# Rounding two hidden rows per VectorE operation instead of one in the second matrix product of a post-norm block

## The reference

```
x = layernorm(x + ssm(x))                      # a diagonal complex state-space layer, 256 states
x = layernorm(x + ffn(x))

def ffn(x):
    h  = rmsnorm(x) * norm_w
    gv = act_quant(h) @ weight_quant(w_gv).T   # 2048 -> 2 x 8192
    value, gate = split(gv)
    h  = value * silu(gate)                    # 8192 wide
    return x + act_quant(h) @ weight_quant(w_out).T     # 8192 -> 2048

def act_quant(a):                              # per row (token)
    scale = 127 / max(|a|)
    return clip(round(a * scale), -127, 127) / scale
```

## Time and profile before

| what | value |
|---|---|
| median of the runs before | 5870.79 us (2 runs, 5864.95 to 5876.63) |
| the profiled execution, its own time | 5864.32 us |
| its span (slowest core, first to last instruction) | 5862.7 us |
| spans of the eight cores | 5836.2 to 5862.7 us |
| granted TensorE clock, mean over the span | 0.810 to 0.812 of full speed on all cores |
| PE busy | 3430.6 us (59%) |
| DVE busy | 2559.8 us (44%), 3497 instructions |
| ACT busy | 1404.7 us (24%) |
| POOL busy | 648.0 us (11%) |

### The profile page before, as it was taken

How to read it: one execution, slowest core, us unless ns; L and a number is a source line. 1 busy time by engine, 2 the same in 40 slices (tenths; PEclk the granted TensorE clock), 3 DMA queues, 4 the chain that set the end, 5 groups by cost and what they waited for, 6 DMA issues and landing times.

```text
span 5862.7 us, 43737 instructions; the slowest of 8 cores (5836.2 to 5862.7 us)
## 1 busy us (share of the span) xinstructions
PE 3430.6 (59%) x13489; PEld 1345.3 (23%) x13489; DVE 2559.8 (44%) x3497; ACT 1404.7 (24%) x1134; POOL 648.0 (11%) x805
## 2 busy tenths in 40 slices
PE   1223421403888787877877799737772574476273
PEld 0110000001333333333333344212231221122121
DVE  1331844746333333333333344487573466268101
ACT  2222122132444444444444433100000000000000
POOL 0210000000000000000000000001112211311314
PEclk9857765756999898988888899868896797788686
DMA  8223345365555455665565522124442443343333
GB/s 223 74 99 108 127 156 169 123 208 163 190 187 190 169 144 136 151 147 133 154 147 132 137 90 92 39 71 131 127 140 81 126 137 97 119 131 122 96 115 106
DMA packets 211695, 774.79 MB, mean 132 GB/s; under 512 B 24412, under 2 KB 61439, under 8 KB 161799
## 3 DMA queue, kind: packets, MB, share of 16 engines
q10 hardware_dynamic: 64512, 318.80, 16.5%
q0 software_dynamic: 68832, 243.32, 15.6%
q1 hardware_dynamic: 78120, 209.87, 12.3%
HBM read 662.83 MB, written 117.44 MB: 133 GB/s over the span
## 4 chain that ended last, share of the span: by engine, by line
DMA 33%; PE 23%; DVE 17%; ACT 11%; issue 10%; POOL 5%; DVEq 1%; ACTq 0%; POOLq 0%; SPq 0%
DMA WOF<-woutT 7%; PE psA L987 6%; DMA WR<-wq2sp 5%; DMA WR<-wgvL 5%; PE psA L784 5%; DMA WOF<-wgvL 5%; PE psB L784 5%; DMA wq2sp<-P 4%; ACT HBF L734 3%; DMA WR<-woutT 3%; ACT P L745 2%; ACT WR L748 2%; PE psB L987 2%; DVE HBF L796 2%; ACT MNA L730 2%
## 5 line engine op out<-in xcount | busy, mean ns | idle before, releaser
L987 PE MATMUL psA<-P,WR 128*128 128x512 bf16 x3072 | 766.3, 410 | 568.7 <-DMA WR<-wq2sp 461.6
L784 PE MATMUL psA<-P,CBF 128*128 128x512 bf16 x2048 | 512.2, 411 | 202.7 <-DVE CBF L738 193.1
L784 PE MATMUL psA<-P,MNA 128*128 128x512 bf16 x2048 | 508.1, 408 | 179.8 <-DVE MNA L738 170.2
L987 PEld LDWEIGHTS psA<-P,WR 128*128 128x128 bf16 x3072 | 308.5, 103 | 1043.2 <-issue 759.3
L784 PE MATMUL psB<-P,CBF 128*128 128x512 bf16 x2048 | 457.4, 379 | 9.6
L784 PE MATMUL psB<-P,MNA 128*128 128x512 bf16 x2048 | 457.4, 379 | 9.6
L752 DVE TENSOR_TENSOR P<-P,WR 128x2048 bf16<-128x2048 bf16 x64 | 78.4, 1225 | 680.7 <-ACT WR L748 680.7
L784 PEld LDWEIGHTS psA<-P,CBF 128*128 128x128 bf16 x2048 | 211.5, 104 | 502.0 <-issue 312.2
L784 PEld LDWEIGHTS psA<-P,MNA 128*128 128x128 bf16 x2048 | 210.1, 104 | 476.2 <-issue 283.7
L987 PE MATMUL psB<-P,WR 128*128 128x512 bf16 x1024 | 248.2, 402 | 82.9 <-DMA WR<-wq2sp 80.8
L398 ACT ACTIVATE WOF<-WOF 128x2048 f32<-128x2048 f32 x96 | 183.5, 1912 | 393.0 <-DMA WOF<-wgvL 252.8
(11 more groups left out here) (217 smaller groups left out, 4096.3 us busy)
## 6 DMA issues: line engine op xcount, KB each, us to landing
P<-wgvL SPq DMA_DIRECT2D x128, 1024.0 KB
WR<-wq2sp POOLq DMA_DIRECT2D x256, 512.0 KB, 4.0
WOF<-woutT ACTq DMA_DIRECT2D x96, 1024.0 KB, 6.2
WOF<-wgvL ACTq DMA_DIRECT2D x64, 1024.0 KB, 5.0
WR<-wgvL ACTq DMA_DIRECT2D x64, 1024.0 KB, 5.1
h2sp<-CBF POOLq DMA_DIRECT2D x128, 256.0 KB, 4.5
WR<-woutT ACTq DMA_DIRECT2D x32, 1024.0 KB, 5.0
wq2sp<-P POOLq DMA_DIRECT2D x64, 512.0 KB, 8.4
```

Source lines behind the costliest of these rows:

```text
L784: sv=sv, last=last: t.matmul(PS[:, (vg * 2 + tq) * 512:(vg * 2 + tq + 1) * 512], WQap(sv + vg)[:, a * 128:(a + 1) * 128], P1[:, a * T + th ...
L987: seg=seg, PSm=PSm: t.matmul(PSm(ds), WR[:, sl * 2048 + jj * 256 + ds * 128: sl * 2048 + jj * 256 + (ds + 1) * 128], P1[:, seg * 16384 + j ...
```

## The change

`d_chain` now takes two blocks, j and j + 1, and is called for every second j. The two DMAs and the two products stay at 512 columns each and are issued one behind the other (DMA, product, DMA, product); the products fill the two halves of one float buffer of 1024 columns. The five rounding operations then run once over 1024 columns. The scratch sets are new (`RNW`: halves of `MNA` and of `WOF`), and the integer copy and its float copy share one memory. `round_neg` is no longer called here. The feeder lists hold 16 pieces for the chains where they held 32, so `d_mm` spreads them and what follows them differently over the groups.

```diff
+    RNW = [
+        (MNA[:, 0:1024], R("MNA", 0, 1024),
+         MNA[:, 1024:2048].bitcast(I32), MNA[:, 1024:2048], R("MNA", 1024, 2048)),
+        (WOF[:, 0:1024], R("WOF", 0, 1024),
+         WOF[:, 1024:2048].bitcast(I32), WOF[:, 1024:2048], R("WOF", 1024, 2048)),
+    ]
+
     def d_chain(q, seg, j):
         par = q % 2
-        jo = seg * 32 + j
-        hq = jo % 8
-        hsl = j % 2
-        b.dma("sync", lambda s, q=q, jo=jo, hq=hq: s.dma_start(
...
-        round_neg(hsl,
-                  P1[:, seg * 16384 + j * 512:seg * 16384 + (j + 1) * 512],
...
+        src_ap, src_r, i_ap, cf_ap, ic_r = RNW[(j // 2) % 2]
+        for h in range(2):
+            jo = seg * 32 + j + h
+            hq = jo % 8
+            b.dma("sync", lambda s, q=q, jo=jo, hq=hq: s.dma_start(
+                out=CBF[:, hq * 512:(hq + 1) * 512],
+                in_=h2sp_t[:, jo, q * 512:(q + 1) * 512]),
+                reads=[("h2sp", jo, q // 2)],
+                writes=R("CBF", hq * 512, (hq + 1) * 512, es=2))
+            b.op("vector", lambda v, hq=hq, h=h, src_ap=src_ap, par=par:
+                 v.tensor_tensor(
+                src_ap[:, h * 512:(h + 1) * 512],
+                CBF[:, hq * 512:(hq + 1) * 512], S2B[par], OP.mult),
+                reads=R("CBF", hq * 512, (hq + 1) * 512, es=2) + S2R[par],
+                writes=src_r)
+        dst_ap = P1[:, seg * 16384 + j * 512:seg * 16384 + (j + 2) * 512]
+        dst_r = R("P1", seg * 16384 + j * 512, seg * 16384 + (j + 2) * 512, es=2)
+        b.op("vector", lambda v: v.tensor_copy(i_ap, src_ap),
+             reads=src_r, writes=ic_r)
+        b.op("vector", lambda v: v.tensor_copy(cf_ap, i_ap),
+             reads=ic_r, writes=ic_r)
+        b.op("vector", lambda v: v.tensor_tensor(src_ap, src_ap, cf_ap,
+                                                 OP.subtract),
+             reads=src_r + ic_r, writes=src_r)
...
     def d_quant(q, seg):
-        for j in range(32):
+        for j in range(0, 32, 2):
             d_chain(q, seg, j)
...
-        f0 = [(lambda q=q, j=j: d_chain(q, 1, j)) for j in range(32)] + tail
+        f0 = [(lambda q=q, j=j: d_chain(q, 1, j)) for j in range(0, 32, 2)] + tail
...
-            f1 = [(lambda q=q, j=j: d_chain(q + 1, 0, j)) for j in range(32)]
+            f1 = [(lambda q=q, j=j: d_chain(q + 1, 0, j)) for j in range(0, 32, 2)]
```

More of the change, by code:

```diff
@@ L935, in d_rowsQ @@
         bcast_row(dqrow, DQR[par], PSB(3), RB(3), DQB[par], DQR[par])
+    RNW = [
[4 more added lines that the diff above has]
+    ]
     def d_chain(q, seg, j):
         par = q % 2
-        jo = seg * 32 + j
-        hq = jo % 8
-        hsl = j % 2
-        b.dma("sync", lambda s, q=q, jo=jo, hq=hq: s.dma_start(
[L943 to L953, removed]
-        round_neg(hsl,
-                  P1[:, seg * 16384 + j * 512:seg * 16384 + (j + 1) * 512],
-                  R("P1", seg * 16384 + j * 512,
-                    seg * 16384 + (j + 1) * 512, es=2))
+        src_ap, src_r, i_ap, cf_ap, ic_r = RNW[(j // 2) % 2]
@@ L959, in d_quant @@
+        b.op("vector", lambda v: v.scalar_tensor_tensor(
+            cf_ap, src_ap, 0.5, cf_ap, OP.is_ge, OP.add),
+            reads=src_r + ic_r, writes=ic_r)
+        b.op("vector", lambda v, dst_ap=dst_ap: v.scalar_tensor_tensor(
+            dst_ap, src_ap, -0.5, cf_ap, OP.is_le, OP.subtract),
+            reads=src_r + ic_r, writes=dst_r)
     def d_quant(q, seg):
-        for j in range(32):
+        for j in range(0, 32, 2):
             d_chain(q, seg, j)
```

## The result

The changed kernel takes 6206.85 us (median of 11 runs) against 5863.4 (median of 10 runs of the kernel before on the same chips), a ratio of 1.0576 with a 95% interval of 1.0551 to 1.06. It is slower by 5.8%; 5.6% was forecast, and 6200 us.

A forecast was written before the change was run, and what follows sets the result against it. Bounds taken: VectorE in stage (0, 0), a loop of engines and weight loads in seg 1, VectorE then GpSimd's order in later stages. 44 + 51 + 84 + 150 = 329 us on 5864 gave 6193; forecast 6200, range 6105 to 6290.

The forecast's parts named there:

- The lag of the odd load: In each pair on VectorE, the second product waits for its load, requested only after the first product: 2.4 to 3.9 us.
- Stage (0, 0): First stage of the last part: VectorE stays the bound, 306 us against 262, +44 us.
- Chains of (q, 0): Stages q = 1 to 3: 18 pairs on VectorE take 177 us against 149, +84 us together.
- Seg 1: Groups of q = 0 to 2: VectorE becomes the bound, 31.0 us a group against 28.6, +51 us together.
- The feeder's split: Stages q = 1 to 3: `d_rowsL` stands behind four groups, not six, so two more come behind the wait: +150 us.
- Rival A: The odd load isn't held up, a pair takes 7.0 us, the new split still costs 150: 5925 us, chance 0.06.
- Rival B: The odd load's lag stays but the split costs nothing, GpSimd's batches overlapping with TensorE: 6050 us, chance 0.07.
- C: VectorE's gain of 1.1 us a pair is passed on in full, without lag or split cost: 5730 us, chance 0.03.
- D: Seg 1's lag of 3.9 us holds everywhere, a pair takes 10.8 us: 6290 us, chance 0.06.

The follow-up runs named there:

- loads_first: The changed kernel with both loads of a pair recorded ahead of both products, new split kept: 5912 us, ratio 1.0069 against the kernel before.
- slots_apart: The changed kernel with its recording order kept, CBF slots dealt out so that a pair's blocks share no region: 5915 us, ratio 1.0074 against the kernel before.
- before_new_split: The kernel before with two 512-column chains in each feeder piece, so the list has the changed kernel's length: 6022 us, ratio 1.0282.
- apply_loads_on_sp: The changed kernel with the apply pieces' loads issued by SP's queue instead of ScalarE's: 6086 us, ratio 1.0334 against the kernel before.
- weights_early: both_fixes_sp with each weight load recorded right behind the matmuls that free its half of WR: 5513 us, ratio 0.935 against the kernel before.
- both_fixes_sp: The changed kernel with a pair's loads first, the feeder's old split and the apply loads on SP: 5705 us, ratio 0.9678 against the kernel before.

## Why the prediction was right

- *The lag of the odd load* (2.4 to 3.9 us by stage, read from SP's waits for the even block): shown. On core 0 the 128 odd products wait 420 us; loads_first and slots_apart take the wait away and with it 295 and 292 us, some 4.7% of the changed kernel's time each. That the cause is the shared region, and not the load's place in the code, is shown by slots_apart.
- *Stage (0, 0)*, +44: measured +47.3. *Chains of (q, 0)*, +84: measured +81.2.
- *Seg 1*, +51: measured +41.4. The mechanism was right and the size a fifth too large. Three figures of that term were off on core 0. The forecast had 217 us for the seven intervals, 651 in three quarters, and 633.6 were measured. From the first addition of a group to the end of its last operation it took 9.5 us, read from one group in which VectorE waited 5.10 us for the residual's load; the changed kernel takes 8.2 on the mean of those 21 groups, 28 us less in all. For two pairs it had 21.6 us, and they take 22.1, 10 us more in all. And it took 200 us for the kernel before in each quarter, 600 in all, where 592.2 were measured. One group of the changed kernel, in the timeline of VectorE on core 0, from its first addition through its last operation to the next group's first addition:

```profile
4146.68 0.69 DVE L1040 TENSOR_TENSOR Z2S<-psA,P 128x512 f32<-128x512 f32 x1
...
4154.31 0.69 DVE L1050 SCALAR_TENSOR_TENSOR Z2S<-CBF,Z2S 128x512 f32<-128x512 f32 x1 [3.93 <-DMA CBF<-x1sp]
...
4177.05 0.68 DVE L1040 TENSOR_TENSOR Z2S<-psB,P 128x512 f32<-128x512 f32 x1
```

The wait of the last operation of a group, in the waits of the kernel before from 3300 us on (sum, count, longest):

```profile
DVE Z2S L1032 <- DMA CBF<-x1sp: 146.6, 32, 6.5
```

The same of the changed kernel from 3700 us on:

```profile
DVE Z2S L1050 <- DMA CBF<-x1sp: 120.4, 32, 5.0
```

The mean over the 32 groups fell from 4.6 us to 3.8. Why this load comes sooner behind the addition was not tried.
- *The feeder's split*, +150: measured +146.3 in the changed kernel, and 2.8% by itself in before_new_split. That the copy in ScalarE's queue lengthens each batch by some 10 us is shown by apply_loads_on_sp (127 us expected between the medians, 6207 to 6080; 121 measured).
- *Rival A* (pair of 7.0 us, split stays, 5925) is what loads_first measures once the odd load no longer waits for the even product: 5912. It was priced rightly and was wrong only in its condition. *Rival B* (the split costs nothing) falls by before_new_split, *C* by the waits of the changed kernel. *D* (3.9 us of lag everywhere) falls by the trace, where the odd products of the first 16 pairs wait 2.5 to 3.1 us on core 0.
- The sum was 329 us over the profiled execution. The medians differ by 343, the medians over cores of the two profiled executions by 330, core 0 by 304. Which of these one compares moves the size by more than any term was off. That 6200 lies within 7 us of 6207 is therefore in part luck: core 0, from whose rows the terms were read, grew by 25 us less than their sum.

## What to carry to other kernels

Making operations wider removes the work that used to stand between dependent steps; before merging, list for each wait what covered it, because a load that is issued only after the step before it can be hidden by nothing once its user moves up to that step. A tracker that works by regions makes neighbours depend on each other where slots are smaller than its granule, and such a dependence can cost next to nothing for long (0.4% here, in the kernel before). And where work is spread by counting pieces, halving the count moves everything listed behind them: here that alone cost 2.8% (1.8 to 3.8).

## What was not expected of the hardware

Loading the weights early raised TensorE's granted clock with nothing done to the matmuls: in the seg 1 groups it went from 0.86 to 0.96 of full speed and from 0.84 to 1.00 (2.4 GHz throughout), in the rows of weights_early and both_fixes_sp above. In the second of these stretches the busy time of about as many matmuls fell from 138.4 to 120.9 us. TensorE stops there for weights about as often as before, but for less time. Its waits in that stretch, first in both_fixes_sp (5392 to 5588), then in weights_early (5260 to 5396):

```profile
PE psA L1007 <- DMA WR<-wq2sp: 41.7, 10, 9.6
PE psB L1007 <- DMA WR<-wq2sp: 16.1, 4, 5.9
```

```profile
PE psA L1019 <- DMA WR<-wq2sp: 11.1, 10, 2.3
PE psB L1019 <- DMA WR<-wq2sp: 4.0, 3, 1.7
```

So part of what a shorter wait brought, some 17 of 60 us in that stretch, came with the clock, a share that the expectation had not priced by itself; the shorter waits themselves are the other 43.
